# Identity products in TensorE's waits, and tripled score products, in a macaron block (MoE, attention, MoE) on one core

## What is computed

```python
x = x + 0.5 * moe(layernorm(x))      # 8 experts, top 2: four MLPs (gelu), four KANs
x = x + attn_block(layernorm(x))     # window attention and a gated FFN
x = x + 0.5 * moe(layernorm(x))      # the same experts again
# moe
logits = x @ gate_W;  rw, sel = top_k(softmax(logits), 2)
h0 = layernorm(x);    basis0 = 1 - tanh((h0[..., None] - grid) * 0.5) ** 2   # 8 hills per value
z = basis0 @ kan_sl_W0;  basis1 = hills(layernorm(z));  kan_out = basis1 @ kan_sl_W1
# attn_block: 16 heads of 8 channels, each row sees itself and the 128 rows before it
scores = q @ k.T * scale;  probs = softmax(mask(scores));  h = x + (probs @ v) @ wo
out = h + (silu(n @ w1) * (n @ w3)) @ w2        # n = layernorm(h)
```

## Time and profile before

| | |
|---|---|
| time before, median of 3 runs | 675.87 us |
| lowest and highest run | 675.67, 681.38 us |
| profiled execution: its time, its span | 682.9, 681.1 us |
| PE busy | 541.0 us, 79% of the span |
| DVE busy | 450.8 us, 66% |
| ACT busy | 373.6 us, 55% |
| mean granted clock, by the records | 0.90 |

### The profile page before, as it was taken

One profiled execution on the slowest core, in us unless ns is written; L12 is line 12 of the kernel. 1 busy time (PEld: TensorE's weight loads), 2 busy tenths in 40 slices (PEclk: granted clock), 3 DMA queues, 4 the chain that ended last, 5 costly groups with the idle time before them and its releaser, 6 DMA issues. The chain is left out here.

```text
span 681.1 us, 18347 instructions
## 1 busy us (share of the span) xinstructions
PE 541.0 (79%) x6060; PEld 470.9 (69%) x6061; DVE 450.8 (66%) x1166; ACT 373.6 (55%) x876; POOL 264.3 (39%) x305
## 2 busy tenths in 40 slices
PE   5347899999997277886999939972489899999960
PEld 4237899999986234664788834672378899999960
DVE  5743778787877496998133384458438688787855
ACT  2335888888944026500555612223358798888930
POOL 6035466666544246700000020120354566666530
PEclk9999999999999779767899978965589999999985
DMA  8972222100100400000000000059610000101106
GB/s 240 370 282 73 64 71 69 31 27 27 28 15 16 132 1 3 2 13 1 16 4 4 5 0 1 0 169 342 268 36 21 27 27 31 31 27 27 24 16 189
DMA packets 41235, 46.51 MB, mean 68 GB/s; under 512 B 7216, under 2 KB 33184, under 8 KB 40160
## 3 DMA queue, kind: packets, MB, share of 16 engines
q1 hardware_dynamic: 32224, 34.00, 15.2%
q0 software_dynamic: 4736, 9.71, 5.2%
q10 hardware_dynamic: 4224, 2.10, 1.0%
HBM read 35.69 MB, written 10.09 MB: 67 GB/s over the span
## 5 line engine op out<-in xcount | busy, mean ns | idle before, releaser
L845 PE MATMUL k_y_ps<-kan_w,k_basis 128*128 x1056 | 127.3, 280 | 8.2 <-DVE k_basis L941 5.7
L845 PEld LDWEIGHTS k_y_ps<-kan_w,k_basis 128*128 128x128 f32 x1056 | 123.9, 196 | 9.9 <-issue 9.8
L835 PE MATMUL k_z_ps<-kan_w,k_basis 128*128 x528 | 119.9, 380 | 1.9 <-issue 1.9
L1107 ACT ACTIVATE k_sig<-k_h1T 128x256 f32<-128x256 f32 x264 | 84.5, 402 | 53.0 <-DVE k_h1T L966 45.3
L835 PEld LDWEIGHTS k_z_ps<-kan_w,k_basis 128*128 128x128 f32 x528 | 97.7, 190 | 14.6 <-issue 2.3
L941 DVE SCALAR_TENSOR_TENSOR k_basis<-k_sig 128x512 f32<-128x512 f32 x132 | 85.8, 691 | 15.7 <-ACT k_sig L1107 13.9
L1100 ACT ACTIVATE k_sig<-k_h0T 128x128 f32<-128x128 f32 x280 | 59.2, 294 | 6.6 <-DVE k_h0T L929 6.6
L1670 ACT ACTIVATE got<-p_ps 128x960 f32<-128x960 f32 (+1 forms) x44 | 39.2, 944 | 27.6 <-PE p_ps L1586 27.6
L661 POOL DMA_INDIRECT y_rows<-k_y,k_rows x33 | 33.2, 1005 | 50.2 <-DVE k_y L973 32.3
L1634 DVE TENSOR_REDUCE p_minus_max<-p_ps 128x6 f32<-128x960 f32 (+1 forms) x44 | 46.2, 1119 | 6.5 <-PE p_ps L1551 5.1
L813 PE MATMUL m_z_ps<-m_xT,m_w 128*128 128x128 f32 x304 | 45.0, 296 | 5.4 <-DVE m_z L989 2.5
(11 more groups left out here) (252 smaller groups left out, 1039.8 us busy)
## 6 DMA issues: line engine op xcount, KB each, us to landing
kan_w<-in_L_ffn_kan_sl_W_dram SPq DMA_DIRECT2D x16, 1024.0 KB, 10.0
x_rows<-got SPq DMA_DIRECT2D x4, 1024.0 KB, 12.4
mlp_w<-in_L_ffn_mlp_W_dram SPq DMA_DIRECT2D x2, 1024.0 KB, 5.8
mlp_w<-in_L_ffn_mlp_W_dram SPq DMA_DIRECT2D x8, 256.0 KB, 6.7
got<-y_rows SPq DMA_DIRECT2D x8, 256.0 KB, 4.9
got<-y_rows ACTq DMA_DIRECT2D x8, 256.0 KB, 5.6
xs<-in_L_attn_x_dram SPq DMA_DIRECT2D x4, 256.0 KB, 3.6
s_cos<-in_cos_dram SPq DMA_DIRECT2D x8, 128.0 KB
```

The lines of the kernel that those rows point to most:

```text
L835: last = nc.tensor.matmul(z_ps, basis0[:, g], k.kan_w0[:, bass.ds(e, 1), g], start=(g == 0), stop=(g == G - 1))
L845: last = nc.tensor.matmul(y_ps, basis1[:, g, c], k.kan_w1[:, bass.ds(e, 1), c, g], start=(g == 0 and c == 0), stop=(g == G - 1 and c == F2 ...
L1107: ins = nc.scalar.activation(sig1[:, g], h1T[:], ACT.Sigmoid, bias=float(-GRID[g]))
```

## The change

A helper `keep_running` multiplies the 128 x 128 identity by itself n times and writes the result to a part of PSUM that nothing reads again. It is called on PE at these places:

- routing (both times): 6 before the first transposition; 10 before the wait for DVE's expert choice; 8 after the sums of counts; then a wait for `in_slot_ready` and 6 more ahead of line 523; 8 after line 523;
- expert blocks (both times): 8 at the start;
- projections: 14 ahead of the first transposition, once the first expert outputs have landed, and 10 at the end;
- attention: 6 between the last row scores and the second turning of the maxima (behind a wait for the maxima of all groups but the last), and 8 at the end;
- finish: 4 after each of the four chunks by wo, 10 after the first transpositions, 8 at the end.

These are 46 in each routing with its expert blocks, 24, 14 and 34: 164 products, 328 records. And in the row scores each group makes the four products of its first key block three times: 8 more for each of 22 groups, 176 products. They write the same values to the same place.

```diff
+def keep_running(nc, k, unused, n):
+    for _ in range(n):
+        nc.tensor.matmul(unused, k.ident[:], k.ident[:], start=True, stop=True)
...
+                keep_running(nc, k, xT_ps[1][:, 0:P], 6)
                 turn(0)
...
+                keep_running(nc, k, xT_ps[0][:, 0:P], 10)
                 pe.wait_ge(up_to_ready, 1)
...
+                keep_running(nc, k, xT_ps[0][:, 0:P], 8)
+                pe.wait_ge(in_slot_ready, 1)
+                keep_running(nc, k, xT_ps[0][:, 0:P], 6)
                 pe.wait_ge(numbers_ready, 2)
...
+                keep_running(nc, k, y_bank[:, 0:P], 8)
                 m_turn(m_x_in[0], m_loaded[0], 1)
...
+                pe.wait_ge(k.got_loaded[0], 16 * TOPK)
+                keep_running(nc, k, nT_ps[1][:, 0:P], 14)
                 chunk_T(0)
...
-                    for i, b in enumerate(blocks):
+                    for i, b in [(0, blocks[0])] * TWICE + list(enumerate(blocks)):
...
+                pe.wait_ge(reduced, 2 * (N - 1))
+                keep_running(nc, k, ps[:, scores_set(N - 2), 0:P], 6)
                 turn_maxima(1)
...
                 for g in range(NCH):
                     by_wo(g)
+                    keep_running(nc, k, T_ps[1][:, 0:P], 4)
                 turn_n2(0)
+                keep_running(nc, k, T_ps[1][:, 0:P], 10)
```

More of the change, by code:

```diff
@@ L1480, in _ @@
                     last.then_inc(v_done, 1)
+                pe.wait_ge(nT_ready, NCH)
+                keep_running(nc, k, nT_ps[1][:, 0:P], 10)
 def attend(nc, k, a, s):
@@ L1504, in attend @@
         HALF = N // 2
+        TWICE = 2
         NC_OUT = T // QC
@@ L1624, in _ @@
                     by_values(t)
+                keep_running(nc, k, ps[:, 0, 0:P], 8)
             @block.vector
@@ L1786, in _ @@
                 by_w2(NCH - 1)
+                pe.wait_ge(nT_ready, NCH)
+                keep_running(nc, k, T_ps[1][:, 0:P], 8)
             @block.scalar
```

## The result

The changed kernel takes 675.03 us (median of 12 runs, 673.67 to 679.26), the one before 677.16 us in the same comparison (12 runs, 675.60 to 681.38). The ratio is 0.995, with a 95% interval from 0.9927 to 0.9973: faster by half a per cent, where 1.2% was forecast. The direction held and the size did not; 675.03 us lies inside the range, and nearer to the rival "the clock gains little" (672.7) than to the forecast.

What follows compares the result with a forecast made beforehand. It took PE's low clock after idle waits to bound four stretches, DVE's maxima the row scores. Terms 0.6 + 0.5 + 1.4 + 2.4 + 2.0 + 0.5 + 1.0 = 8.4 us, 675.87 - 8.4 = 667.5 us; range 660.5 to 676.

Steps and rivals of the forecast that it cites:

- the clock gains little: Rival, whole kernel: filled waits keep holes, gather bound by the weight stream, routing gives nothing; gain 3.2, 672.7 us; chance 0.30.
- Projections (taken 0.6): Projections: q and k at full clock remove DVE's 0.96 us wait for k; gain 0.6 us, bounds 0 and 1.0.
- Row scores (taken 0.5): First turning of the maxima: full clock shortens DVE's 0.69 us wait; gain 0.5 us, bounds 0 to 0.7.
- Key scores (taken 1.4): Key scores: 4.5 us of PE at low clock becomes some 2.3; gain 1.4 us, bounds 0.4 to 2.5.
- Finish (taken 2.4): Finish: 0.9 us from the first chunk by wo, 1.5 from later PE work; gain 2.4 us, bounds 0.4 and 3.5.
- Routing 2 (taken 2.0): Second routing: gather issued 2.9 us earlier, landing earlier by 0 to all of it; gain taken 2.0 us.
- The term of the list inversion (0.4): List inversion in the second routing: full clock gains 0.4 us, bounds -0.8 to 1.1.
- Routing 1 (taken 0.5): First routing: as in the second, but DVE's normalising paces the transpositions; gain 0.5 us, bounds -0.8 and 1.5.
- Start of the expert blocks (taken 1.0): Start of both expert blocks: first products at full clock, 0.5 us each; gain 1.0 us, bounds 0 and 1.8.
- All holds: Rival, projections onward: clock stays full, gather lands as much earlier as issued; 13.3 to 14.8 us, 661 to 662.5; chance 0.12.
- The row scores become PE's: Rival, row scores: at low clock a group takes 2.8 us for 2.1; 15.4 us slower, 691; chance 0.06.
- The identity products do not count: Rival, all filled waits: zeros and ones may be light work for the clock; slower, 678 us; chance 0.04.

Runs made afterwards that it cites:

- a_again: The changed kernel once more, with assertions on the loaded counts; 677.04 us, 0.9972 of the kernel before.
- key_fill: The changed kernel with seven more identity products behind the first group of key scores, in PE's wait for the first exponentials; 0.9945 of the kernel before.
- scores_only: The kernel before with only the tripled score products of each group's first key block, no identity products; 680.80 us, 1.0044 of the kernel before.
- finish_only: The kernel before with only the identity products of the finish; 678.81 us, 1.0000 of the kernel before.
- best_two: The changed kernel without tripled score products, plus 7 identity products behind first key scores, 22 for 10 in the finish, 10 at each last KAN block; 0.9877 of before.
- best_again: best_two unchanged, run again in another comparison; 0.9878 of the kernel before.
- after_light: The changed kernel with a mask on each loaded count in place of assertions; 0.9969 of the kernel before.
- after: The changed kernel as first measured and traced; 675.03 us, 0.995 of the kernel before.
- b_again: The kernel before once more, with only assertions on the loaded counts added; 679.78 us, 1.0017 of the kernel before.
- fill_transposed: The changed kernel with each identity product replaced by a transposition of the identity; 685.24 us, 1.0091 of the kernel before.

## Why the forecast was right in direction and wrong in size

Most of the forecast's signs came in the trace: the clock of 1.00 in the row scores with DVE's maxima unbroken, DVE's wait in the finish at 1.54 us (forecast 1.6), its wait in routing 2 at 3.41 (some 3), the gather issued 2.65 us earlier (2.9). One did not: w1 and w3 ran at 1.92 us a pair at first, not 1.02. Term by term:

*Projections (taken 0.6).* q begins 1.5 us after the first transposition, in place of 2.0. In the traced execution it is at the full clock from its first record and DVE's wait of 0.96 us is gone; in a_again q begins at 2.08 us a pair and the wait is 0.94, as before the change. The stage is 30.6 and 30.7 us, 0 to 0.5 less than before in all: inside the bounds, at the low end, and the wait that the term was made of is worth about 0.1 us.

*Row scores (taken 0.5).* 1.4 to 1.7 us with the turning. DVE's wait of 0.69 us is 0.34, and the six products keep the clock full through the second turning. Right in kind, and under-sized: it lies above the bounds of 0 to 0.7.

*Key scores (taken 1.4).* -1.2, +0.2 and -0.4 us. **This step failed.** I read the 0.16 us by which the exponentials waited as proof that PE was nearly on time there, and did not ask what PE's gain would turn into: the table load of ACT holds the first exponential, and a faster first group is a longer wait behind it. I had even named the pause ("it may fall once more") and priced it as a smaller gain, where it takes all. key_fill, with the wait filled, has 70.8 us, a gain of 2.2 against 73.0, inside the bounds of 0.4 to 2.5. So the price of the low clock was right, and the step that failed is what was said of the wait.

*Finish (taken 2.4).* DVE's wait for the first chunk fell from 2.46 to 1.54 us, the 0.9 forecast. The rest gained 0.9 or 2.6 us, as the clock fell or not in the unfilled half of the wait. Inside the bounds, with both cases seen. The 0.9 rests on a slip: a third of 4.48 + 0.6 is 1.7 us, 4.48 / 3 + 0.6 is 2.1, and the forecast has 1.9; that it fits to 0.1 us is luck.

*Routing 2 (taken 2.0).* The logits came 2.7 us earlier after the barrier: DVE's wait of 6.16 us is

```profile
453.26 0.29 DVE L333 TENSOR_REDUCE top<-logit_ps 128x16 f32<-128x128 f32 x1 [3.41 <-PE logit_ps L515]
```

The six products took 1.41 us at the full clock and cost 0.9. The sums gained 0.1, not 0.5: DVE waits for ACT's probabilities instead. **The term of the list inversion (0.4) was mis-sized**: it gained nothing, -0.2.

```profile
466.96 5.83 PE L534 MATMUL found_ps<-numbers,in_row 128*128 128x96 f16 x32
...
475.16 1.06 POOL L483 DMA_INDIRECT m_x_in<-x_rows,rows_of  x1 [22.33 <-DVE k_rows_first L426]
```

The 32 products took 5.79 us at the low clock and 5.83 with 3.4 us of it at the full one (window 468.4 to 471.8 us). The gather was issued 2.65 us earlier after the barrier (30.0 against 32.65 us) and landed 6.07 us later, as before (6.11), while the weight stream still ran: its last packets came 3 us after the landing, where before the stream ended with it. From the last w2 to the landed gather it is 1.9 to 2.7 us less (table): the 2.0 was right. Behind the landing up to 0.9 us went again, in the wait for the first w1 (1.6, 0.8 and 1.6 us in place of 0.9 and 1.2). The rival "the gather is bound by the stream" is out at this place. The Trainium skill, DMA: Bandwidth & Descriptors, Queues, rings and completion order, says that an engine takes its queues in turn by packets; this trace agrees, in that the landing followed the issue by 6.07 us with the stream still running.

*Routing 1 (taken 0.5).* The logits were not earlier by 0.01 us, and the gather was issued at 40.63 us (40.62 before). It landed 0.4 us earlier all the same, but that is its own scatter: in the twenty traces it lands 4.0 to 6.9 us after its issue here. So no gain is shown. DVE's normalising sets the pace, as the prediction said.

*Start of the expert blocks (taken 1.0).* This can't be told. With the same instructions in it the second expert stretch varied by 6.4 us, between scores_only and finish_only:

```profile
488.48:683.40 194.92, 166.29 (x1157) 157.23 (x1156) 135.30 (x322) 136.91 (x353) 99.39 (x119) 0.91 0.15 41
```

```profile
486.84:675.30 188.46, 160.93 (x1157) 152.27 (x1156) 135.27 (x322) 137.02 (x353) 99.10 (x119) 0.94 0.15 42
```

The numbers of records agree, and DVE and ACT to 0.1 us; PE has 5.4 us less at a clock of 0.94 in place of 0.91. In scores_only the clock stood at 0.50 also from 530.6 to 533.8 and from 656.8 to 663.5 us, with PE busy 3.20 of 3.20 and 6.10 of 6.70 us. These are two programs on two chips; but best_two and best_again are one program, and their expert stretches took 381.9 and 387.7 us. What makes the clock fall inside a stretch of one execution and not of another is open. The prediction's reading that the long inner parts run at the full clock holds: 1.00 from 55 to 220 and from 497 to 656 us in the kernel before.

*The sum, and what it was set against.* **The step that failed most was the last: "It is 7.0 us above the median; I take the same difference from the median."** The traced execution of the kernel before lay 5.7 us above the median of its twelve runs, that of the changed kernel 0.5 under its own; of the 8.4 us between the traces these distances are 6.3, and 2.1 are left. The terms were read where the clock was low in one execution, and taken as if a filled stretch kept it full in all. 3.3 us of the 8.4 between the two traces stand in the expert stretches, which vary by more than that. And the clock's falls are not at the same places each time. In the 12 executions of the changed kernel the mean clock goes from 0.920 to 0.942: the three at 0.939 to 0.942 have spans of 672.3 to 673.0 us, the three at 0.920 to 0.922 of 675.1 to 677.4. The traced one has 0.942. (The clock is not all of it: the two shortest spans, 671.9 and 672.2, have 0.932 and 0.931.) For a_again and after_light too the traced execution had one of the highest clocks of its twelve (0.942 of 0.922 to 0.942, 0.932 of 0.920 to 0.934), 4.4 and 3.5 us under their median spans, so the stage lengths in the table flatter the change. As a rough estimate, outside the expert stretches a_again, after_light and after gain 1.8, 3.2 and 3.8 us on b_again (295.7 less 288.3, 287.8 and 290.2, less the distances of both traces from their medians: 5.6, 4.7 and 1.7), in accord with 0.5%. It puts the whole of these distances down to the stages outside the expert stretches, which is not shown. In which stages the median execution lost what the traced ones kept stays open, since it was not traced.

*The rivals.* "All holds" did not come. "The row scores become PE's" came in scores_only, for a few groups. "The identity products do not count" is refuted by the clock of 1.00; for transpositions it fits what fill_transposed shows. "The clock gains little" was nearest in time, with the wrong reason for routing 2. Two of the forecast's numbers do not follow from its own terms. A group of row scores at the low clock would take 1.98 + 1.1 + 0.25 = 3.3 us, not 2.8, so that rival's price would be some 26 us, not 15.4. And the two slower rivals, 691 and 678 us, have 0.10 together, while the text leaves 0.08 above 676.

## What to carry to other kernels

Filler products pay for certain only if they reach to the end of the wait: a wait that is half filled lost the clock in its second half in five traces of nine here, and a filled stretch that ends early against another engine's fixed work makes a new unfilled wait. Ask of each term what the engine that is now early will wait for. And where single executions of a program differ by more than the change, a sum from one trace is the difference of two draws: take its terms from stages whose lengths repeat, and discount the rest.

## What the runs showed of the hardware

- Transpositions of the identity left the clock at 0.50: 3.25 us of them at 232.90, and eight unbroken microseconds together with the logits in routing 2. Ordinary products of the same shape, in the same place, raised it 4.3 us after the first of them.
- 32 float16 products of 96 columns took 5.79 us at the low clock and 5.83 with 3.4 us of it at the full one.
- Gaps of 1.3 to 2.1 us stood amid the 128-record runs of small products where a packet of the instruction queue fell in the run (three gaps in two kernels, at the full clock); 14 products more, ahead of it, moved the packets behind the runs, and the gaps were gone. So it seems that PE waited for its own program; the profile does not name the cause.
- The second expert stretch, with the same instructions, took 188.5 and 194.9 us in two kernels, at a mean clock of 0.94 and 0.91; one and the same program took 381.9 and 387.7 us for both stretches.
- A gather issued into a running weight stream landed 6.07 and 6.11 us later in the traces of the changed kernel and of the one before, whether 3 us of the stream were left behind it or none (5.4 to 6.6 in all twenty traces).
